# Attention on one Trainium2 core: softmax denominators by GpSimd adds and accumulating DMAs, value blocks for two steps at a time

## The chip, the cores and the metric

The kernel runs on one NeuronCore of a Trainium2 chip. The metric is the device time of one execution in microseconds (us). The kernel before has three timed runs: 3693.86, 3694.41 and 3703.93 us, median 3694.41.

## What is computed

The whole kernel is a graph attention layer followed by a transformer block on x of shape (2, 2048, 512), float32. The change touches the transformer's attention alone: 2 batches, 16 heads of 32 columns, sequences of 2048, softmax over all 2048 keys.

```python
def attention(h, Wqkv, bqkv, Wproj, bproj):
    qkv = (h @ Wqkv + bqkv).reshape(B, L, 3, H, HD)
    q, k, v = jnp.moveaxis(qkv, 2, 0)
    attn = jax.nn.softmax(jnp.einsum('blhd,bmhd->bhlm', q, k) * HD ** (-0.5), axis=-1)
    return jnp.einsum('bhlm,bmhd->blhd', attn, v).reshape(B, L, D) @ Wproj + bproj
```

## The kernel before

The program runs in phases with barriers between them: setup, graph layer, query/key/value projection, attention (`attention_phase`, line 926), output projection, MLP. Queries and keys arrive in DRAM as a high and a low float32r part (`qk_d`), so that one matmul over 3 x 32 rows gives a product of full precision.

**Groups, halves, steps.** The attention goes over 16 groups of two heads of one batch. A group has two halves of 1024 queries; a half has 16 steps of 128 keys, so a group has 32 steps (`ST`). A step computes four score tiles of 128 keys x 512 queries (two heads, two columns of queries; line 1261) into three PSUM banks `pS` used in turn. ScalarE takes the exponential of each into `prob` (line 1104), four buffers of 128x4x512 (`PR`). TensorE multiplies the values with the four tiles into one PSUM bank `pO`, four column groups of 32 (line 1228, `values`). This is a float32 product, which the trace records as eight matmuls for a block of four.

**Maxima.** The exponential needs the maximum of each query's row. So all scores are also computed the other way around, queries on the partitions, 128 tiles a group (line 1213, `maxima`), into three PSUM banks `pM`; VectorE reduces each (line 1147). These tiles belong to the next group and run 6 steps ahead of it (`LEAD`): each score matmul is followed by one maxima matmul. At step 26 VectorE takes the top of each row (line 1151), TensorE turns it (line 1219), VectorE splits it (lines 1158 and 1160), and SP sends it into two rows of `qs` (`rows`, line 1038), where it is part of the next group's contraction. TensorE begins a group only when these rows have landed (line 1267). The last group has no maxima beside it after its first steps.

**Denominators.** Of the 16 steps of a half, 11 (`ADDED`, line 944) are added up by GpSimd into `acc`: ten additions of 128x2048 (line 1083). The other five (`SUMMED`) go through TensorE, which multiplies them with a matrix of ones into the PSUM bank `pZ` right behind their values (line 1234, called from `behind`, line 1280). At step 2 of the next half (`FINISH`) the accumulator goes the same way (`finish`, line 1238). ScalarE copies the bank to `rec` (line 1133), VectorE inverts it in four pieces of 128 columns (line 1169, steps 4 to 7) and multiplies it with the copy `oc` of the values' bank (lines 1119 and 1177). ScalarE's queue stores the product with four DMAs (line 1126).

**Order and queues.** Each engine works its instructions in the order written. On TensorE a step is three scores with maxima, then the values of the step before (`behind`), then the fourth score. ScalarE may reuse a `prob` buffer once its values and its addition are done (`free`, line 1088). SP issues the loads of a group's queries and keys into one of four buffers (`U`, lines 1025 and 1028) when the group before has ended, the values' load (line 1032), and the rows. The 16 groups are written as four groups, a loop of two turns of four, and four groups (`groups`, line 1005).

Of the kernel before, what the change touches and what calls it, by code (L numbers as in the profile page):

```python
# [5 lines left out]
F32 = mybir.dt.float32  # L6
# [6 lines left out]
P = 128  # L13
B = 2
# [911 lines left out]
def attention_phase(nc, io, keep):  # L926

    with ExitStack() as ctx:
# [6 lines left out]
        MS = NM // ST  # L938
        LEAD = 6
        EARLY = MS  # L940
        U = 4
        PR = 4

        ADDED = [0, 1, 2, 4, 5, 6, 8, 9, 11, 12, 13]
        NA = len(ADDED) - 1
        FINISH = 2
        INVERT = 4
        STORE = 10
        SUMMED = [t for t in range(MT) if t not in ADDED]
# [14 lines left out]
        zero = m.sb("zero", [P, 1])  # L964
# [6 lines left out]
        top_ready, nm_hi, step_done, added, o_done, o_copied = [  # L971
            m.sem(x) for x in ("top_ready", "nm_hi", "step_done", "added", "o_done", "o_copied")]
        z_done, z_read, inverted, o_ready = [m.sem(x) for x in ("z_done", "z_read", "inverted", "o_ready")]
        top_rows = m.sems("top_rows", U)
        block = m.block()
# [6 lines left out]
        def m_unit(g, step, c):  # L982


            ahead = 1 if step < ST - LEAD else 2
            return (g + ahead, (step + LEAD) % ST * MS + c) if before(g, NG - ahead) else None

        def turn(g):


            return g * (NM + 1) + NM + (EARLY if before(g, NG - 1) else 0)

        def tile(g, n):

            return g * (NM + 1) + n - (1 if n < EARLY and at_least(g, 1) else 0)

        def bank(g, n):
            return pM[(n - (1 if n < EARLY and at_least(g, 1) else 0)) % 3]

        def turned(g):  # L1000

            return pM[(NM + (EARLY if before(g, NG - 1) else 0)) % 3]
        assert (NM + 1) % 3 == 0

        def groups(eng, body):


            for g in range(U):
                body(g, g, lambda j: (g + j) // 2)
            with eng.Fori(1, NG // U - 1) as i:  # L1010
                for k in range(U):
                    body(i * U + k, k, lambda j: i * (U // 2) + (k + j) // 2)
# [758 lines left out]
```

## Time and profile before

| | |
|---|---|
| median of three runs | 3694.41 us |
| span of the profiled execution | 3696.8 us |
| instructions | 51173 |
| busy, whole span: TensorE, VectorE, ScalarE, GpSimd | 93%, 61%, 42%, 48% |
| attention, first exponential to last score | some 990 to 2790 us |

The profile gives the span of the profiled execution, from its first to its last instruction; a time of its own around that span is not recorded, so the span is set against the median, from which it differs by 2.4 us. PE is TensorE, DVE VectorE, ACT ScalarE, POOL GpSimd, and SP the engine that only issues DMAs; a name with q behind it (SPq) is that engine's own queue. Matmuls are pipelined: each is shown longer than the distance to the next, so the distance between starts is the price of one. "Idle before" is what the engine stood still for in front of a group, with what ended it.

### The profile page before, as it was taken

How to read it: one execution, taken by the hardware profiler on the slowest of the kernel's cores; microseconds unless marked ns; L12 is line 12 of the kernel's file. 1: busy time of each engine (PE TensorE's matmuls, PEld its weight loads, DVE VectorE, ACT ScalarE, POOL GpSimd, SP SyncE). 2: the span in 40 equal slices, each digit the busy share in tenths (PEclk: the TensorE clock that was granted, in tenths of full speed). 3: DMA queues.
4: the chain of work that ended last, by engine and by line, in shares of the span. 5: the costliest groups of instructions: out<-in, count | busy, mean ns of one | idle time of the engine just before them, and what ended most of it. 6: DMA issues, size and time to landing. Idle time of an engine off the chain costs nothing. (4 is left out here: it accounts for less than half of the span.)

```text
span 3696.8 us, 51173 instructions
## 1 busy us (share of the span) xinstructions
PE 3452.4 (93%) x17516; PEld 2197.3 (59%) x17516; DVE 2266.1 (61%) x3547; ACT 1552.4 (42%) x2751; POOL 1775.8 (48%) x527
## 2 busy tenths in 40 slices
PE   7899996997999999999999999999995779999999
PEld 6488885775544444444444444444434658888887
DVE  1378874444978788788788887887715932222222
ACT  0111114341166666666656666666662242222222
POOL 1033321001288788787887887877885500000000
PEclk9999998997699999999999999999997889999999
DMA  4122224446201222102222022200004641111100
GB/s 163 66 93 88 91 80 172 172 158 183 46 17 34 43 47 44 38 16 44 47 48 44 7 44 47 47 10 13 7 6 154 216 146 68 40 40 40 37 32 23
DMA packets 158137, 250.59 MB, mean 68 GB/s; under 512 B 46939, under 2 KB 68699, under 8 KB 151774
## 3 DMA queue, kind: packets, MB, share of 16 engines
q1 hardware_dynamic: 147166, 230.96, 21.1%
q10 hardware_dynamic: 10752, 16.79, 1.5%
q8 instruction: 128, 2.10, 0.2%
q14 instruction: 91, 0.75, 0.1%
HBM read 158.89 MB, written 88.08 MB: 67 GB/s over the span
## 5 line engine op out<-in xcount | busy, mean ns | idle before, releaser
L1147 DVE TENSOR_REDUCE att_mx<-att_pM 128x1 f32<-128x512 f32 x2048 | 1267.9, 680 | 336.2 <-PE att_pM L1213 334.0
L1104 ACT ACTIVATE att_prob<-att_pS 128x512 f32<-128x512 f32 x2048 | 1080.4, 601 | 772.8 <-PE att_pS L1261 765.2
L1083 POOL TENSOR_TENSOR att_acc<-att_acc,att_prob 128x2048 f32<-128x2048 f32 x288 | 1327.5, 4609 | 129.2 <-ACT att_prob L1104 104.1
L1213 PE MATMUL att_pM<-att_ks,att_qs 96*128 96x512 f32 x2048 | 855.1, 432 | 54.7 <-DVE att_mx L1147 33.6
L1261 PE MATMUL att_pS<-att_qs,att_ks 98*128 98x512 f32 x2048 | 868.8, 430 | 10.2 <-ACT att_prob L1104 8.0
L1261 PEld LDWEIGHTS att_pS<-att_qs,att_ks 98*128 98x128 f32 x2048 | 386.2, 190 | 555.1 <-ACT att_prob L1104 385.7
L1228 PE MATMUL att_pO<-att_prob,att_V 128*32 128x512 f32 x4096 | 548.7, 608 | 0.7 <-ACT att_prob L1104 0.7
L1213 PEld LDWEIGHTS att_pM<-att_ks,att_qs 96*128 96x128 f32 x2048 | 405.4, 198 | 200.5 <-DVE att_mx L1147 120.3
L1627 DVE TENSOR_TENSOR mlp_us<-mlp_tu,mlp_us 128x512 fp32r<-128x512 f32 x128 | 89.7, 700 | 536.0 <-ACT mlp_us L1600 536.0
L1670 PE MATMUL mlp_pu<-mlp_hs,mlp_W 128*128 128x512 f32 x1536 | 370.7, 391 | 18.9 <-DVE mlp_W L1619 18.9
L1689 PE MATMUL mlp_pa<-mlp_W,mlp_us 128*128 128x512 f32 x1536 | 368.8, 389 | 0.0
L1670 PEld LDWEIGHTS mlp_pu<-mlp_hs,mlp_W 128*128 128x128 f32 x1536 | 289.7, 189 | 79.4 <-issue 19.2
L1612 POOL TENSOR_TENSOR mlp_hs<-mlp_hf,mlp_hs 128x512 fp32r<-128x512 f32 x32 | 41.1, 1287 | 598.6 <-ACT mlp_hs L1578 598.6
L1689 PEld LDWEIGHTS mlp_pa<-mlp_W,mlp_us 128*128 128x128 f32 x1536 | 288.5, 188 | 59.7
L1599 ACT ACTIVATE mlp_tu<-mlp_pu,keep_cols 128x512 f32<-128x512 f32 x128 | 88.2, 689 | 503.4 <-PE mlp_pu L1670 503.4
L1083 POOL TENSOR_TENSOR att_acc<-att_prob 128x2048 f32<-128x2048 f32 x32 | 146.6, 4580 | 291.5 <-ACT att_prob L1104 291.5
L921 PE MATMUL qkv_pq<-qkv_hs,qkv_W 128*128 128x512 f32 x768 | 187.3, 400 | 2.4 <-DVE qkv_hs L861 2.4
L1169 DVE RECIPROCAL att_rec<-att_rec 128x128 f32<-128x128 f32 x128 | 119.6, 940 | 105.3 <-ACT att_rec L1133 105.3
L1228 PEld LDWEIGHTS att_pO<-att_prob,att_V 128*32 128x32 f32 x4096 | 81.0, 108 | 166.6 <-issue 93.2
L1234 PE MATMUL att_pZ<-att_prob,att_ones 128*32 128x512 f32 x1280 | 166.6, 592 | 0.0
L921 PEld LDWEIGHTS qkv_pq<-qkv_hs,qkv_W 128*128 128x128 f32 x768 | 144.9, 192 | 32.4 <-issue 2.8
L1062 POOL MEMSET att_ones<- 128x32 f32 x1 | 0.1, 124 | 304.8 <-POOLq L107 304.8
(181 smaller groups left out, 2984.7 us busy)
## 6 DMA issues: line engine op xcount, KB each, us to landing
qk_d<-qkv_qs SPq DMA_DIRECT2D x64, 512.0 KB, 2.7
att_qs<-qk_d SPq DMA_DIRECT2D x48, 512.0 KB, 7.4
att_ks<-qk_d SPq DMA_DIRECT2D x48, 512.0 KB, 13.8
gat_xT<-in_xT SPq DMA_DIRECT2D x32, 256.0 KB, 3.1
gat_xrow<-in_x SPq DMA_DIRECT2D x32, 256.0 KB, 2.8
x_d<-gat_x SPq DMA_DIRECT2D x32, 256.0 KB, 2.1
qkv_xr<-x_d SPq DMA_DIRECT2D x8, 1024.0 KB, 5.8
v_d<-qkv_vs SPq DMA_DIRECT2D x32, 256.0 KB, 2.0
```

The source lines that it names most:

```text
L921: last = nc.tensor.matmul(out[:], a, r, start=n + c == 0, stop=n == 2 and c == DC - 1)
L1083: nc.gpsimd.tensor_tensor(acc[half][:], old[:], new[:], ALU.add).then_inc(added, 1)
L1104: nc.scalar.activation(prob[step % PR][:, c, :], pS[n % 3][:], ACT.Exp, scale=SCALE).then_inc(exp_done, 1)
L1147: nc.vector.tensor_reduce(mx[:, n // 4, n % 4:n % 4 + 1], bank(g, n)[:], AX.X, ALU.max).then_inc(m_read, 1)
L1169: nc.vector.reciprocal(rec[:, at], rec[:, at]).then_inc(inverted, 1)
L1213: nc.tensor.matmul(bank(g, n)[:], qs[k][0:KD, h, t * P:(t + 1) * P], ks[k][0:KD, h, mc * 512:(mc + 1) * 512], start=True, stop=True).then_ ...
L1228: last = nc.tensor.matmul(pO[c * HD:(c + 1) * HD, :], V[k % 2][:, mt, (c // 2) * HD:(c // 2 + 1) * HD], prob[step % PR][:, c, :], start=mt ...
L1234: last = nc.tensor.matmul(pZ[c * HD:(c + 1) * HD, :], ones[:], src[:, c, :], start=first, stop=last_one, skip_group_check=True)
L1261: nc.tensor.matmul(pS[n % 3][:], ks[k][:, h, mt * P:(mt + 1) * P], qs[k][:, h, lc * 512:(lc + 1) * 512], start=True, stop=True).then_inc(s ...
L1627: nc.vector.tensor_tensor(us[j % 2][:, 1, :], tu[j % 2][:], us[j % 2][:, 0, :], ALU.subtract).then_inc(u_lo, 1)
L1670: last = nc.tensor.matmul(pu[j % 4][:], W1[:, k, c, j * P:(j + 1) * P], hs[s][:, w, c, :], start=q + c == 0, stop=q == 2 and c == DC - 1)
L1689: last = nc.tensor.matmul(pa[nt][:], us[j % 2][:, k, nt * P:(nt + 1) * P], W2[:, w, j, :], start=j + q == 0, stop=j == MC - 1 and q == 2)
```

## The change

It does this, all in `attention_phase`:

- The steps of a half that TensorE summed are gone. Six steps of 16 (`SENT`: 2, 4, 6, 8, 10, 12) are summed by DMAs into a new tile `gathered`: the first by a plain copy on SP's queue (`send_first`), the other five by accumulating DMAs that GpSimd issues (`send`), each waiting for the one before. GpSimd adds the other ten steps (nine additions of 128x2048). `finish` moves from step 2 to step 4 of the next half and puts both `gathered` and `acc` through the ones, into a bank of the scores' turn; `pZ` goes.
- The reciprocal is packed: after ScalarE's copy SP moves one row for each of four column groups into `packed` (128x16), VectorE inverts this (step 6), SP writes it to a small DRAM tensor `z_d` and reads it back spread over 32 partitions each (`reciprocals`).
- The product with the values moves from VectorE to GpSimd (`scale`, after its fifth addition), the stores from ScalarE's queue to SP's.
- TensorE does the values of two steps together, every second step, behind the third score.
- The maxima have four PSUM banks instead of three. `prob` has eight buffers instead of four, `qs` and `ks` three each instead of four.
- The groups are written out without a loop, with constants for every wait.

```diff
+        U = 3
+        PR = 8
+        SENT = [2, 4, 6, 8, 10, 12]
+        ADDED = [t for t in range(MT) if t not in SENT]
+        FINISH = 4
+        INVERT = 6
+        SCALED = 5
...
+        gathered = m.sb("gathered", [P, 4, 512])
+        packed = m.sb("packed", [P, 16])
-        pM = [m.ps(f"pM{i}") for i in range(3)]
-        pO, pZ = m.ps("pO"), m.ps("pZ")
+        pM = [m.ps(f"pM{i}") for i in range(4)]
+        pO = m.ps("pO")
...
+            def send_first(n):
+                step = n % 2 * MT + SENT[0]
+                sp.wait_ge(exp_done, exps(n // 2, step))
+                if n >= 1:
+                    sp.wait_ge(exp_done, turns_of[n - 1] + 1)
+                sp.dma_start(gathered[:], prob[step % PR][:]).then_inc(first_sent, 16)
+            def reciprocals(n):
+                sp.wait_ge(exp_done, turns_of[n] + 1)
+                for c in range(4):
+                    row = rec[c * HD:c * HD + 1, :].rearrange("a (i x) -> a i x", x=16)
+                    sp.dma_start(packed[c * HD:(c + 1) * HD, :], row).then_inc(z_packed, 16)
+                sp.wait_ge(inverted, n + 1)
+                sp.dma_start(io["z_d"][n % 2].rearrange("c (i x) -> (c i) x", x=16), packed[:]).then_inc(z_kept, 16)
+                sp.wait_ge(z_kept, 16 * (n + 1))
+                for c in range(4):
+                    sp.dma_start(rec[c * HD:(c + 1) * HD, :], io["z_d"][n % 2, c:c + 1, :].to_broadcast([HD, 512])).then_inc(z_spread, 16)
...
+            for g in range(NG):
+                if g >= 1:
+                    sp.wait_ge(step_done, g * ST)
+                    if g + 2 < NG:
+                        load(g + 2)
+                    if g + 1 < NG:
+                        load_v(g + 1)
+                    send_first(2 * g)
+                    reciprocals(2 * g - 1)
+                    store(2 * g - 1)
+                else:
+                    send_first(0)
+                send_first(2 * g + 1)
+                reciprocals(2 * g)
+                store(2 * g)
+                if g + 1 < NG:
+                    rows(g + 1)
...
+            def send(n, j):
+                step = n % 2 * MT + SENT[j]
+                pool.wait_ge(exp_done, exps(n // 2, step))
+                if j == 1:
+                    pool.wait_ge(first_sent, (n + 1) * 16)
+                else:
+                    pool.wait_ge(sent, (n * (len(SENT) - 1) + j - 1) * 16)
+                nc.gpsimd.dma_start(gathered[:], prob[step % PR][:], accum_op=ALU.add).then_inc(sent, 16)
...
+                        nc.gpsimd.tensor_tensor(acc[half][:], old[:], new[:], ALU.add).then_inc(added, 1)
+                        if ADDED[i] - 1 in SENT[1:]:
+                            send(n, SENT.index(ADDED[i] - 1))
+                        if i == SCALED and n >= 1:
+                            pool.wait_ge(added, n * NA + i)
+                            scale(n - 1)
...
+            def finish(n):
+                at = turns_of[n]
+                pe.wait_ge(exp_done, at - 2)
+                pe.wait_ge(sent, (n + 1) * (len(SENT) - 1) * 16)
+                sums(pS[at % 3], gathered, True, False)
                 pe.wait_ge(added, (n + 1) * NA)
-                sums(acc[(step // MT - 1) % 2], False, True).then_inc(z_done, 1)
+                sums(pS[at % 3], acc[n % 2], False, True).then_inc(s_done, 1)
...
+                    for c in range(4):
+                        scores(g, step, c)
+                        if c == 2 and step % 2 == 0 and (g or step):
+                            behind(*divmod(g * ST + step - 2, ST))
+                            behind(*divmod(g * ST + step - 1, ST))
+                            if step % MT == FINISH and (g or step >= MT):
+                                finish(2 * g + step // MT - 1)
```

## Rows read from the trace of the kernel before

**Rows 1.** The page's part 1: busy time, share of the span, instructions.

```profile
PE 3452.4 (93%) x17516; PEld 2197.3 (59%) x17516; DVE 2266.1 (61%) x3547; ACT 1552.4 (42%) x2751; POOL 1775.8 (48%) x527
```

**Rows 2.** Windows, 1278 to 1390 us: busy by engine, clock, DMA share.

```profile
1278.00:1390.00 112.00, 109.66 (x605) 53.55 (x601) 91.20 (x141) 69.67 (x131) 91.08 (x21) 1.00 0.18 39
```

**Rows 3.** Timeline of ACT: copies of the values' bank, start and duration.

```profile
1101.85 0.60 ACT L1119 ACTIVATE att_oc<-att_pO 128x512 f32<-128x512 f32 x1 [0.64 <-PE att_pO L1228]
...
1214.90 0.60 ACT L1119 ACTIVATE att_oc<-att_pO 128x512 f32<-128x512 f32 x1 [0.64 <-PE att_pO L1228]
...
1838.03 0.60 ACT L1119 ACTIVATE att_oc<-att_pO 128x512 f32<-128x512 f32 x1 [0.59 <-PE att_pO L1228]
...
1898.32 0.60 ACT L1119 ACTIVATE att_oc<-att_pO 128x512 f32<-128x512 f32 x1 [1.49 <-PE att_pO L1228]
...
2634.16 0.60 ACT L1119 ACTIVATE att_oc<-att_pO 128x512 f32<-128x512 f32 x1 [0.53 <-PE att_pO L1228]
...
2785.24 0.60 ACT L1119 ACTIVATE att_oc<-att_pO 128x512 f32<-128x512 f32 x1 [1.19 <-PE att_pO L1228]
```

**Rows 4.** Timeline of PE, 1829.90 to 1834.84 us, maxima left out.

```profile
1829.90 1.06 PE L1228 MATMUL att_pO<-att_prob,att_V 128*32 128x512 f32 x8
1830.90 0.50 PE L1261 MATMUL att_pS<-att_qs,att_ks 98*128 98x512 f32 x1
...
1831.47 0.39 PE L1261 MATMUL att_pS<-att_qs,att_ks 98*128 98x512 f32 x1
...
1831.94 0.40 PE L1261 MATMUL att_pS<-att_qs,att_ks 98*128 98x512 f32 x1
...
1832.41 0.41 PE L1261 MATMUL att_pS<-att_qs,att_ks 98*128 98x512 f32 x1
...
1832.98 1.06 PE L1228 MATMUL att_pO<-att_prob,att_V 128*32 128x512 f32 x8
1833.86 1.04 PE L1234 MATMUL att_pZ<-att_prob,att_ones 128*32 128x512 f32 x8
1834.84 0.50 PE L1261 MATMUL att_pS<-att_qs,att_ks 98*128 98x512 f32 x1
```

**Rows 5.** Groups by line (busy, mean ns), and tile att_o (ns min/median/max).

```profile
L1169 DVE RECIPROCAL att_rec<-att_rec 128x128 f32<-128x128 f32 x128 | 119.6, 940 | 105.3 <-ACT att_rec L1133 105.3
...
L1612 POOL TENSOR_TENSOR mlp_hs<-mlp_hf,mlp_hs 128x512 fp32r<-128x512 f32 x32 | 41.1, 1287 | 598.6 <-ACT mlp_hs L1578 598.6
...
L1177 DVE TENSOR_TENSOR att_o<-att_oc,att_rec x32: 692/3036/4677, 1072.8 to 2796.1; 128x512 f32<-128x512 f32 x32
```

**Rows 6.** Timeline: runs on ACT, DVE and POOL, start and duration.

```profile
1803.56 2.06 ACT L1104 ACTIVATE att_prob<-att_pS 128x512 f32<-128x512 f32 x4 [1.01 <-PE att_pS L1261]
...
1804.11 2.42 DVE L1147 TENSOR_REDUCE att_mx<-att_pM 128x1 f32<-128x512 f32 x4
...
1854.36 23.51 POOL L1083 TENSOR_TENSOR att_acc<-att_acc,att_prob 128x2048 f32<-128x2048 f32 x5 [2.09 <-ACT att_prob L1104]
```

**Rows 7.** DMA issues (KB, us to landing), and GB/s in 2800 to 2830.

```profile
att_ks<-qk_d SPq DMA_DIRECT2D x48, 512.0 KB, 13.8
...
o_d<-att_o ACTq DMA_DIRECT2D x128, 64.0 KB, 1.7
...
prj_xr<-x_d SPq DMA_DIRECT2D x8, 1024.0 KB, 10.4
x_d<-prj_x SPq DMA_DIRECT2D x8, 1024.0 KB, 5.3
...
att_qs<-att_nm SPq DMA_DIRECT2D x32, 16.0 KB, 2.1
...
GB/s 0 0 66 243 298 415 306 404 410 412 352 363 382 415 402 374 309 407 366 344 380 380 412 393 186 33 0 0 0 0 0 0 0 22 0 0 0 0 0 0
```

**Rows 8.** Timeline, 2791 to 2801 us: the attention phase's end.

```profile
2791.92 0.60 ACT L1133 ACTIVATE att_rec<-att_pZ 128x512 f32<-128x512 f32 x1 [6.09 <-PE att_pZ L1234]
...
2800.90 0.37 SPq L1335 DMA_DIRECT2D prj_stage<-in_Wproj  x1
```

More of the change, by code:

```diff
@@ L980, in attention_phase, with m_tile @@
         o_v = io["o_d"].rearrange("(g h p) (b n) -> g h p b n", h=2, p=HD, b=B)
-        def m_unit(g, step, c):
+        def m_tile(g, step, c):
             ahead = 1 if step < ST - LEAD else 2
-            return (g + ahead, (step + LEAD) % ST * MS + c) if before(g, NG - ahead) else None
-        def turn(g):
[L991 to L1012, printed above, removed]
-            for g in range(NG - U, NG):
-                body(g, g % U, lambda j: (g + j) // 2)
@@ L1016, in half_before, with fill @@
-        def half_before(g, step):
-            return 2 * g + step // MT - 1
+            return (g + ahead, (step + LEAD) % ST * 4 + c) if g + ahead < NG else None
+        place = {}
+        def fill(what):
+            place[what] = len(place)
+        for q in range(NM):
+            fill((0, q))
+        for q in range(EARLY):
+            fill((1, q))
+        fill("turned 0")
+        for q in range(EARLY, LEAD * 4):
+            fill((1, q))
+        for g in range(NG):
+            for step in range(ST):
+                if step == ST - LEAD + 1 and g + 1 < NG:
+                    fill(f"turned {g + 1}")
+                for c in range(4):
+                    if m_tile(g, step, c):
+                        fill(m_tile(g, step, c))
@@ new lines, in attention_phase, with score_turn, exps @@
+        turns_of = {}
+        def score_turn(what):
+            turns_of[what] = len(turns_of)
+        for g in range(NG):
+            for step in range(ST):
+                for c in range(4):
+                    score_turn((g, step, c))
+                    if c == 2 and step % MT == FINISH and (g or step >= MT):
+                        score_turn(2 * g + step // MT - 1)
+        score_turn(2 * NG - 1)
+        def exps(g, step):
+            return turns_of[g, step, 3] + 1
+        def turn(g):
+            return place[f"turned {g}"]
@@ new lines, in _ @@
+            load(0)
+            load(1)
+            load_v(0)
+            load_v(1)
+            load(2)
+            rows(0)
+            for g in range(NG):
+                if g >= 1:
+                    sp.wait_ge(step_done, g * ST)
+                    if g + 2 < NG:
[12 more added lines that the diff above has]
+                    rows(g + 1)
@@ L1060, in _ @@
+            reciprocals(2 * NG - 1)
+            store(2 * NG - 1)
+            for x in o_stored:
+                sp.wait_ge(x, 16 * 4 * NG)
         @block.gpsimd
@@ L1269, in body @@
+            for q in range(NM):
+                maxima(0, q)
+            for q in range(EARLY):
+                maxima(1, q)
+            top_of(0)
+            for q in range(EARLY, LEAD * 4):
+                maxima(1, q)
+            pe.wait_ge(cleared, 1 + U)
+            for g in range(NG):
+                pe.wait_ge(top_rows[g % U], (g // U + 1) * 32)
+                pe.wait_ge(v_loaded[g % 2], (g // 2 + 1) * 16)
                 for step in range(ST):
-                    if step == ST - LEAD + 1 and before(g, NG - 1):
+                    if step == ST - LEAD + 1 and g + 1 < NG:
```

331 lines of the change are left out of this document (144 added, 187 removed).

## The prediction

> **What bounds the kernel now.** I read the busy times of the page first: TensorE has work in 93% of the span [rows 1]. Busy is not yet bound, so next came the windows. In a 112 us stretch of the attention loop TensorE is busy 109.7 us, VectorE 91.2, GpSimd 91.1 and ScalarE 69.7, at full clock [rows 2]. TensorE is first there and two others are close enough to take over.
>
> The copies of the values' bank (one for each half group, 32 in all) give the rhythm: 1214.90 - 1101.85 = 113.05 us for a group, **56.5 us for a half** of 16 steps. One half, around 1898, took 60.3 us; the last three together took 151.1 us, without maxima for most of them [rows 3]. From 1101.85 to 2634.16 lie 27 halves, 1532.3 us, which is 27 x 56.5 and some 6 to 7 more; with the half before 1101.85 I count 28 of full rhythm.
>
> The timeline of TensorE shows what a half is made of [rows 4]. A plain step is 1832.98 - 1829.90 = 3.08 us: values to first score 1.00, first to second score 0.57, two more at 0.47 (each with a maxima matmul between), last score to values 0.57. So in a run a score with its maxima costs 0.47, and a change of kind adds 0.10 behind the first score and 0.10 ahead of the values. Values followed by ones matmuls take 0.88 instead of 1.00, the ones 0.98. A half is then 16 x 3.08 = 49.3, plus five ones blocks of 0.86 (4.3), plus one closing block of some 1.1: 54.7. The other 1.8 us are VectorE's: a reciprocal of 0.94 us [rows 5] on top of four maxima (2.42 us, 0.605 each [rows 6]) makes 3.36 us, over the 3.08 of a step, four times (1.1 us); and the product that ends the half takes 3.04 us in the median where it can take 0.69 [rows 5].
>
> GpSimd adds at 23.51 / 5 = 4.70 us and still waits for ScalarE before its runs [rows 6], so it does not bind now.
>
> **The change, part by part.**
>
> *TensorE.* Values now come for two steps at a time: eight scores with maxima, then two value blocks. Gap by gap: 0.57 + 6 x 0.47 + 0.57 + 0.88 + 1.00 = 5.84 us for two steps, 46.7 for a half. The five ones blocks go; the closing one becomes two (accumulator and gathered block): 2 x 0.98, less 0.12 because the values before them are followed by their own kind. **TensorE's path: 48.6 us** [rows 4]. Two conditions: eight maxima at 0.605 are 4.84 us and eight exponentials at 2.06 / 4 = 0.515 are 4.12 [rows 6], both inside 5.84. Within the run, maxima leave TensorE every 0.47 and VectorE takes 0.605: the eighth tile asks for its bank at 7 x 0.47 = 3.3 us, and the fourth of four banks is read at some 0.4 + 4 x 0.605 = 2.8, so four banks cover it; with three it would be the fifth tile's read, 3.4, a small stall. That is what the freed bank is worth, some 0.1 us a run, and the sum has no such stall.
>
> *VectorE.* Four reciprocals of 0.94 us become one of 128x16, and the product leaves: 3.8 + 3.0 us a half off an engine that then holds 64 x 0.605 = 38.7. It is out of the race.
>
> *GpSimd.* Ten adds become nine: 9 x 4.70 = 42.3. It takes the product: the nearest row is a 128x512 operation of two inputs on this engine, 1.29 us [rows 5]. It issues five accumulating DMAs. No row has an issue on this engine. From below 0.37 us, an issue on SP's queue [rows 8]; from above the 1.29 of the small product, since this engine would write the transfer's list as it works through a tile. I take 1.0, nearer to the row of the same engine: 5.0. **GpSimd's own work: 48.6 us**, as much as TensorE's.
>
> *The chain of accumulating DMAs.* This decides. Each of the five waits for the landing of the one before, and the wait stands in GpSimd's own order, so it holds back the adds behind it. The order is add 1, 3, 5, send, add 7, send, add 9, send, product, add 11, send, add 13, send, add 14, 15. Between first and last send are four intervals, each as long as the larger of the landing L and about 5.7 (add plus issue; 7.0 once, with the product). Outside are five adds, 23.5, and one issue, 1.0. So **a half is at least 24.5 + 4 L**. It equals TensorE's 48.6 at L = 6.0, and today's 56.5 at L = 8.0. No row has a DMA from SBUF to SBUF, nor one that adds. Bounds: 1024 KB plain, one way, lands in 5.3 us (store in the projection); in a crowd, 10.4 [rows 7]. A value from rows: an addition must read both operands, 2.1 MB; the best slices of the projection's start move 412 to 415 GB/s [rows 7], which makes 5.1 us, and the 64 KB store's 1.7 us less its own 0.2 is the fixed part: L = 6.6. I take that, since it is nearer to the 5.3 of the same size on an empty queue than to the crowded 10.4. Then a half is 24.5 + 26.4 = **50.9 us**, 5.6 less than now.
>
> *SP's queue.* It gets the first plain copy of a half (1 MB, landing 5.3), four packing DMAs, one to DRAM, four back, the stores, and, behind those, the top rows of the next group. A small DMA lands in 2.1 us [rows 7]. The first copy goes at step 4 behind the closing sums, lands two steps later and is asked for after add 5, 14.1 us behind them: hidden. The three hops of the denominators (some 9 us with issues) end before the product, which waits for the third send: hidden. The top rows come last: product done 14.1 + 2 x 6.6 + 2 x 1.0 + 1.3 = 30.6 us behind the closing sums, four stores and two row DMAs issued at 0.37 each, landing 2.1: 34.9; TensorE comes to the next group after 11.3 steps x 2.92 = 33.0 us. It would wait 1.9 us a group. That costs nothing while GpSimd is last, as TensorE has 2.3 us to spare each half; with that cover gone it is 15 x 1.9 = 28 us. The same holds for the key and query loads, which crowd the queues for the first five steps of a group and may lengthen the last send.
>
> *Three buffers for keys instead of four, eight for probabilities instead of four.* The load for group g+2 starts at the start of g and is asked for 26 steps (some 75 us) later; its pieces of 512 KB land in 13.8 us in the median [rows 7]. Nothing. Eight blocks let GpSimd be late by up to four steps more, which it needs.
>
> *Loops written out.* The long half of 60.3 is where the loop turns, 3.8 us over the rhythm; with its entry and exit it is the 7 us over 27 x 56.5 [rows 3]. They go.
>
> **Sum, against the span of 3696.8**, which is 2.4 us over the median of 3694.4: 28 halves x 5.6 = -157; loop edges -7; first half, where GpSimd is not yet late, -8; last three halves 3 x 50.9 = 152.7 against 151.1, +2; the end: sums to the next phase's first load takes 2800.90 - 2791.92 = 9.0 us now [rows 8], and the reciprocals' 3.5 are replaced by three hops with issues (about 9) and a slower product, +7. Together -163: 3534 against the span, **3531** against the median.
>
> **The rivals.**
> 1. *The DMAs are quick and nothing of the chain shows (L up to 6).* TensorE and GpSimd tie at 48.6: 28 x 7.9 = -221, -7, -8, last three 145.8 against 151.1 -5, end +7: -234, so 3460. For it: no DRAM at either end, so L may lie at the 5.3 of the plain store. Against: two operands to read. The Trainium skill ("DMA: Bandwidth & Descriptors", Anatomy of one DMA) gives 2.0 us plus the bytes at 436 GB/s for a DMA of this queue, 4.4 us for 1 MB, which would put the kernel into this case; this trace's plain megabyte took 5.3, and no run so far has an accumulating one.
> 2. *Slower: the chain outgrows the half.* Place: GpSimd's wait ahead of each send. If the two operands are read one behind the other at the pace of one plain megabyte, L = 1.7 + 2 x (5.3 - 1.7) = 8.9 and the half is 60.1: 28 x 3.6 = +101, last three 180.3 against 151.1 +29, loop edges -7, end +7: 3824. It decides from L = 8.0 up. For it: each landing comes with an issue by GpSimd of unknown price, and loads share the engines once a group. Against: TensorE saves nothing that this takes until L passes 8.
> 3. *The work moved off TensorE was hidden anyway.* Then the time would stay. Against: TensorE's idle in a steady half is 2% [rows 2], so its 5 blocks are on the path. Only a mix near L = 8 gives no change.
>
> **Chances.** Forecast (chain binds, L 6.0 to 7.8, time 3470 to 3670): 0.40. Rival 1: 0.31. Rival 2: 0.25. No change: 0.04. A difference under about 0.3% (11 us) can't be told from none here. Faster 0.71, same 0.04, slower 0.25. The range goes from 3450 (rival 1, with the loop edges and a little more) to 3770 (a half of 58.5, L = 8.5), which leaves out the worst of rival 2, some 0.15.
>
> **What would show it.** Copies of the values' bank 51 us apart instead of 56.5. On TensorE pairs of value blocks, 5.84 us from pair to pair where nothing waits, and no ones matmuls on probabilities. On GpSimd: sends 6.6 us apart, its idle time ahead of the adds put down to a DMA; TensorE waiting at the closing sums of each half for GpSimd. VectorE under 40 us busy a half. If sends stand under 6 us apart and TensorE never waits, rival 1 holds; over 8, rival 2. The forecast would be wrong at its root if TensorE's pairs took over 6.1 us, or if GpSimd's adds slowed beside the DMAs from 4.70.

## The result, and the profile after

The changed kernel takes 3750.6 us in the median of four runs (3742.9 to 3758.5), the kernel before 3699.2 in the runs beside it: ratio 1.0135, 95% interval 1.0113 to 1.0157. It is slower by 1.4%, where 3531 and a gain were forecast. The time lies inside the stated range (3450 to 3770), near its upper end, but on the other side of the kernel before: the forecast gain did not come. The one that comes near is rival 2.

The page's first part, and the line of its second part that shows the granted clock of TensorE in tenths, to be read against [rows 1]:

```profile
PE 3334.6 (89%) x16492; PEld 2225.5 (59%) x16492; DVE 2056.1 (55%) x3419; ACT 1527.7 (41%) x2751; POOL 1800.3 (48%) x685
...
PEclk8999998997699999999899999999987889999999
```

TensorE's share falls from 93% to 89% while the span grows: it waits. The window of one group in the middle of the attention (columns as in [rows 2]) says the same; the DMA engines' share goes from 0.18 to 0.68.

```profile
1795.10:1911.30 116.20, 104.32 (x546) 55.80 (x546) 79.74 (x133) 68.42 (x133) 93.72 (x31) 0.94 0.68 150
```

The copies of the values' bank, as in [rows 3]:

```profile
1795.06 0.60 ACT L1186 ACTIVATE att_oc<-att_pO 128x512 f32<-128x512 f32 x1 [2.94 <-PE att_pO L1286]
...
1850.52 0.60 ACT L1186 ACTIVATE att_oc<-att_pO 128x512 f32<-128x512 f32 x1 [1.31 <-PE att_pO L1286]
...
1911.27 0.60 ACT L1186 ACTIVATE att_oc<-att_pO 128x512 f32<-128x512 f32 x1 [2.78 <-PE att_pO L1286]
```

The two halves take 55.5 and 60.8 us. Over 26 halves, from the copy at 1102.60 to the one at 2611.24, a half takes **58.0 us** in the mean, against 56.8 for the same 26 before. The difference of the two spans can be added up from this. By its second copy the attention is 0.8 us later, 26 x 1.25 = 32.5 us come in these halves, 2.9 in the last four, and the stretch from the last copy to the next phase's first load grows from 15.7 to 36.2 us, by 20.5. The phases behind give back 2.7. The sum is 54.0, as 3750.8 - 3696.8.

TensorE's timeline, maxima left out as in [rows 4]:

```profile
1887.67 0.50 PE L1316 MATMUL att_pS<-att_qs,att_ks 98*128 98x512 f32 x1
...
1891.89 1.92 PE L1286 MATMUL att_pO<-att_prob,att_V 128*32 128x512 f32 x16
1893.75 0.50 PE L1316 MATMUL att_pS<-att_qs,att_ks 98*128 98x512 f32 x1
...
1897.69 1.92 PE L1286 MATMUL att_pO<-att_prob,att_V 128*32 128x512 f32 x16
1899.54 0.50 PE L1316 MATMUL att_pS<-att_qs,att_ks 98*128 98x512 f32 x1
...
1906.08 0.50 PE L1316 MATMUL att_pS<-att_qs,att_ks 98*128 98x512 f32 x1 [3.93 <-DMA att_qs<-att_nm]
...
1928.35 1.94 PE L1292 MATMUL att_pS<-att_gathered,att_ones 128*32 128x512 f32 x8 [5.55 <-ACT att_prob L1203]
```

The new order runs as worked out: 3.94 us from the first score of a run to the values (3.96), 1.85 for two value blocks (1.88), 5.79 from pair to pair (5.84). But at 1906.08 TensorE has stood 3.93 us for the top rows, and at 1928.35 another 5.55 ahead of the closing sums, behind ScalarE. Its own work is short enough; something else sets the half.

Behind such a wait TensorE also runs slower for a while. Two stretches of 4 us, at and behind an earlier wait of the changed kernel (TensorE busy, granted clock, DMA share, GB/s):

```profile
1807.00:1811.00 4.00, 0.00 (x0) 1.00 1.06 221
1811.00:1815.00 4.00, 3.80 (x17) 0.57 0.97 205
```

The clock falls from the upper of its two levels (2.4 GHz, shown as 1.00) towards the lower (1.2 GHz, 0.50) behind 4 us without a matmul. Over 1102 to 2550 us its mean is 1.00 before and 0.94 now. The next timeline shows why this does not set the half either. It is GpSimd's:

```profile
1880.34 0.86 POOL L1134 DMA_DIRECT2D att_gathered<-att_prob  x1
1880.95 4.89 POOL L1154 TENSOR_TENSOR att_acc<-att_acc,att_prob 128x2048 f32<-128x2048 f32 x1
1888.51 0.89 POOL L1134 DMA_DIRECT2D att_gathered<-att_prob  x1 [2.67 <-DMA att_gathered<-att_prob]
...
1896.02 0.88 POOL L1134 DMA_DIRECT2D att_gathered<-att_prob  x1 [2.02 <-ACT att_prob L1203]
1896.63 1.59 POOL L1124 TENSOR_TENSOR att_o<-att_oc,att_rec 128x512 f32<-128x512 f32 x1
...
1903.79 0.88 POOL L1134 DMA_DIRECT2D att_gathered<-att_prob  x1 [0.87 <-DMA att_gathered<-att_prob]
...
1911.28 0.87 POOL L1134 DMA_DIRECT2D att_gathered<-att_prob  x1 [2.05 <-DMA att_gathered<-att_prob]
1911.89 9.64 POOL L1154 TENSOR_TENSOR att_acc<-att_acc,att_prob 128x2048 f32<-128x2048 f32 x2
...
1936.11 4.58 POOL L1154 TENSOR_TENSOR att_acc<-att_acc,att_prob 128x2048 f32<-128x2048 f32 x1 [5.28 <-ACT att_prob L1203]
1940.64 0.87 POOL L1134 DMA_DIRECT2D att_gathered<-att_prob  x1
```

Sends start at 1880.34, 1888.51, 1896.02, 1903.79 and 1911.28, some 7.5 to 8.2 us apart. An issue followed by an add is over in 5.5 (1880.34 to 1880.95 to 1885.8), and then GpSimd stands. The profile puts one of these waits down to the landing of the send before (2.67), another to ScalarE (2.02). The landing times show that it is the landing each time: in 126 of the 128 intervals of the trace the next send starts 0.53 to 0.56 us behind the landing of the one before, whichever the profile names. A later TensorE or ScalarE therefore does not lengthen these intervals. Over the 26 halves counted above, the four intervals of a half have means of 8.2, 8.0, 8.0 and 7.7 us. From the last send of a half to the first of the next pass 24.3 us inside a group and 27.9 across a group's start. Together that is the half of 58.0. The last halves, with no key or query load beside them, come nearest to a floor: 7.5, 7.5, 7.8, 7.5 and 24.2, **54.5 us**.

The DMAs of the changed kernel (KB, median us from issue to landing, over the kernel), and two of its waits (us in total, times, longest):

```profile
att_gathered<-att_prob POOLq DMA_DIRECT2D x160, 1024.0 KB, 7.2
...
att_gathered<-att_prob SPq DMA_DIRECT2D x32, 1024.0 KB, 4.7
...
o_d<-att_o SPq DMA_DIRECT2D x128, 64.0 KB, 4.7
...
ACT att_prob L1203 <- DMA att_gathered<-att_prob: 172.7, 53, 9.4
POOL att_gathered L1134 <- DMA att_gathered<-att_prob: 161.5, 79, 4.5
```

The 64 KB stores, 1.7 us on ScalarE's queue before [rows 7], take 4.7 on SP's. What the DMA engines carry beside a send shows in its landing. Of the 104 sends inside these 26 halves that another send follows, 43 had under 100 KB of SP's transfers beside them and landed in 7.0 us in the mean, and 30 with more of these landed in 7.5. With a packet of the queue that the profile calls q8 instruction beside them, 18 took 7.8, and 13 that met both took 8.2. This is a sorting of one trace, not a test.

The half that crosses into a new group is different. Here are SP's queue, ScalarE, and the landing of the last send of that half (columns of the three: start, duration, or KB and us to landing):

```profile
1898.25 4.18 SPq L1059 DMA_DIRECT2D o_d<-att_o  x4
1902.48 1.19 SPq L1050 DMA_DIRECT2D att_qs<-att_nm  x2
1911.26 1.28 SPq L1038 DMA_DIRECT2D att_qs<-qk_d  x3
1912.59 1.84 SPq L1040 DMA_DIRECT2D att_ks<-qk_d  x3
```

```profile
1927.70 1.57 ACT L1203 ACTIVATE att_prob<-att_pS 128x512 f32<-128x512 f32 x3 [7.62 <-DMA att_gathered<-att_prob]
```

```profile
att_gathered<-att_prob POOLq DMA_DIRECT2D x1, 1024.0 KB, 16.3
```

The top rows go out at 1902.48, behind the stores, and TensorE waits for them. It comes to the new group at 1906; with that the loads of keys and queries start, at 1911.26, in the same moment as the last send at 1911.28. That send takes 16.3 us instead of 7.2. ScalarE may not overwrite its block before, stands 7.62 us, and GpSimd's third add of the next half begins 5.28 late. In the 13 crossings that have such loads this send lands in 12 to 17 us, 15.0 in the mean.

The end of the phase:

```profile
2821.39 0.60 ACT L1186 ACTIVATE att_oc<-att_pO 128x512 f32<-128x512 f32 x1 [1.19 <-PE att_pO L1286]
...
2843.00 2.41 SPq L1074 DMA_DIRECT2D att_packed<-att_rec  x4
...
2857.60 0.41 SPq L1387 DMA_DIRECT2D prj_stage<-in_Wproj  x1
```

From the copy of the values' bank to the copy of the sums (2842.38) pass 21.0 us, where it was 6.7 before: GpSimd has two sends and three additions left when TensorE has finished the values, and nothing covers them here.

### The profile page after: what moved, and what is told of

It reads as the page before. It is cut to its first block and busy times, and to the rows that moved or that the text cites. A ratio compares the mean times of both kernels' runs of the same rounds, so it can differ in the third digit from the quotient of the medians.

```text
span 3750.8 us, 44693 instructions
## 1 busy us (share of the span) xinstructions
PE 3334.6 (89%) x16492; PEld 2225.5 (59%) x16492; DVE 2056.1 (55%) x3419; ACT 1527.7 (41%) x2751; POOL 1800.3 (48%) x685
## 3 DMA queue, kind: packets, MB, share of 16 engines
q1 hardware_dynamic: 174814, 281.84, 24.5%
## 5 line engine op out<-in xcount | busy, mean ns | idle before, releaser
L1218 DVE TENSOR_REDUCE att_mx<-att_pM 128x1 f32<-128x512 f32 x2048 | 1254.7, 681 | 517.9 <-PE att_pM L1271 517.4
L1203 ACT ACTIVATE att_prob<-att_pS 128x512 f32<-128x512 f32 x2048 | 1054.1, 615 | 718.6 <-PE att_pS L1316 542.3
L1154 POOL TENSOR_TENSOR att_acc<-att_acc,att_prob 128x2048 f32<-128x2048 f32 x256 | 1204.8, 4706 | 56.0 <-ACT att_prob L1203 39.7
L1316 PEld LDWEIGHTS att_pS<-att_qs,att_ks 98*128 98x128 f32 x2048 | 394.3, 193 | 472.1 <-issue 203.1
L1286 PE MATMUL att_pO<-att_prob,att_V 128*32 128x512 f32 x4096 | 524.8, 632 | 0.0
L1271 PEld LDWEIGHTS att_pM<-att_ks,att_qs 96*128 96x128 f32 x2048 | 414.7, 203 | 154.9 <-DVE att_mx L1218 78.1
L1134 POOL DMA_DIRECT2D att_gathered<-att_prob x160 | 139.9, 875 | 282.2 <-DMA att_gathered<-att_prob 161.5
L1286 PEld LDWEIGHTS att_pO<-att_prob,att_V 128*32 128x32 f32 x4096 | 110.7, 113 | 266.3 <-ACT att_prob L1203 136.8
L1513 PE MATMUL prj_pp<-prj_W,prj_os 128*128 128x512 f32 x384 | 99.1, 422 | 49.0 <-POOL prj_os L1462 49.0
```

Source lines behind the costliest of these rows:

```text
L1134: nc.gpsimd.dma_start(gathered[:], prob[step % PR][:], accum_op=ALU.add).then_inc(sent, 16)
L1154: nc.gpsimd.tensor_tensor(acc[half][:], old[:], new[:], ALU.add).then_inc(added, 1)
L1203: nc.scalar.activation(prob[step % PR][:, c, :], pS[at % 3][:], ACT.Exp, scale=SCALE).then_inc(exp_done, 1)
L1218: nc.vector.tensor_reduce(mx[:, q // 4, q % 4:q % 4 + 1], bank(at)[:], AX.X, ALU.max).then_inc(m_read, 1)
L1271: nc.tensor.matmul(bank(at)[:], qs[k][0:KD, h, t * P:(t + 1) * P], ks[k][0:KD, h, mc * 512:(mc + 1) * 512], start=True, stop=True).then_in ...
L1286: last = nc.tensor.matmul(pO[c * HD:(c + 1) * HD, :], V[g % 2][:, mt, (c // 2) * HD:(c // 2 + 1) * HD], prob[step % PR][:, c, :], start=mt ...
```

## The experiments

Each one is an edit of the changed kernel; the diffs show their main lines. There are two theories. **C**: the chain of accumulating DMAs sets the half, and the loads lengthen its last link. **R**: the rows' place on SP's queue is what costs. Ratios are to the kernel before, run beside.

**e1: rows ahead of the stores.**

```diff
                 reciprocals(2 * g)
-                store(2 * g)
                 if g + 1 < NG:
                     rows(g + 1)
+                store(2 * g)
```

> The changed kernel with one thing moved on SP's queue: the top rows of the next group go out ahead of the stores. In the changed kernel's trace TensorE stands 83.8 us in all for these rows at the 15 group starts. Theory R (the rows' place on the queue is the loss, what turns a half of 56.6 into one of 58): those waits go and the kernel takes about 3700 us. Theory C (the half is set by GpSimd's chain of sends, the loads at a group's start lengthening the last one): the waits for the rows go, but TensorE waits as long at the closing sums instead, and the time stays within 15 us of 3750.

Measured: 3818.3 us, ratio 1.0323 (1.0300 to 1.0347). Slower by 68 us than with the rows late, which neither theory had. TensorE's waits for the rows are gone, and the halves alternate between 55.2 and 65.4 us, where the changed kernel's do between 56.7 and 59.3. SP's queue and GpSimd's fourth and fifth send of one crossing show why:

```profile
1817.36 1.43 SPq L1038 DMA_DIRECT2D att_qs<-qk_d  x3
1818.83 1.67 SPq L1040 DMA_DIRECT2D att_ks<-qk_d  x3
...
1818.72 0.87 POOL L1134 DMA_DIRECT2D att_gathered<-att_prob  x1 [0.92 <-DMA att_gathered<-att_prob]
1819.33 4.88 POOL L1154 TENSOR_TENSOR att_acc<-att_acc,att_prob 128x2048 f32<-128x2048 f32 x1
1836.48 0.88 POOL L1134 DMA_DIRECT2D att_gathered<-att_prob  x1 [12.27 <-DMA att_gathered<-att_prob]
```

TensorE now starts the group earlier and brings the loads along: they go out at 1817.4 to 1820.5, around the fourth send at 1818.72, and not at the fifth. GpSimd waits 12.27 us for its landing, and the fifth follows after 17.8 us instead of 7.5 (10.7 to 18.1 in the 13 groups with loads). The fifth itself, which the loads hit in the changed kernel, has adds behind it before the next send is due. On this reading the late rows had been shielding the chain in the changed kernel. R falls. C had forecast a time within 15 us of 3750 and missed it too; that the rows act as a switch for when the loads come is an explanation made after the run, and e5 tests it.

**e2: loads apart from the chain.** The queries' and the keys' loads now wait for different sends; `load` issues either.

```diff
                     sp.wait_ge(step_done, g * ST)
+                    sp.wait_ge(sent, 2 * g * (len(SENT) - 1) * 16)
                     if g + 2 < NG:
-                        load(g + 2)
+                        load(g + 2, (0,))
...
+                sp.wait_ge(sent, (2 * g + 1) * (len(SENT) - 1) * 16)
+                if g >= 1 and g + 2 < NG:
+                    load(g + 2, (1,))
                 send_first(2 * g + 1)
```

> The changed kernel with the key and query loads moved: the queries and values of a group wait on SP for the last send of the half before, the keys for the last send of the next half, so that no load shares the DMA engines with that send. Theory C: the last send of every second half lands in 7 to 8 us instead of 16, ScalarE no longer waits some 7 us a group for its buffer, a group crossing costs 24.3 us from last to first send instead of 27.7: 15 x 3.4 = 50 us less, 3700. Against it: the first copy of a half then queues behind the loads and the first send comes later, which gives the gain back (3750 or more). Theory R: no gain, since the rows are as late as before.

Measured: 3702.0 us, ratio 1.0004 (0.9990 to 1.0017); 49 us less than the changed kernel, as expected. The gap from last to first send is 24.3 us in every half now; the mean half is 55.9 instead of 58.0. So the loads' meeting with the last send is worth 49 us, nearly the whole loss against before (51).

**e3: sends as plain copies.** The kernel leaves out the five additions inside the DMAs of a half, so each send overwrites `gathered` and five of the six sent steps are missing from the denominators (the expectation says four).

```diff
-                nc.gpsimd.dma_start(gathered[:], prob[step % PR][:], accum_op=ALU.add).then_inc(sent, 16)
+                nc.gpsimd.dma_start(gathered[:], prob[step % PR][:]).then_inc(sent, 16)
```

> The changed kernel with the five sends of a half as plain copies: the addition inside the DMA is left out (so the denominators lack four steps of a half), number, size, issuing engine and waits stay. Theory C: a plain megabyte lands in 4.7 to 5.3 us, under the 5.6 of an add and an issue, so the chain drops out; sends stand 5.7 us apart (7.5 once, with the product), a half falls from 58 to 49 or 51 and the time to 3480 to 3540. If what holds the half is not the length of the chain but the number of DMAs or GpSimd's work, the time falls by less than 60 us.

Measured: 3506.6 us, ratio 0.9481 (0.9458 to 0.9503). The landing of the sends, and the windows of a half inside a group and one across:

```profile
att_gathered<-att_prob POOLq DMA_DIRECT2D x160, 1024.0 KB, 4.7
...
1847.90:1896.20 48.30, 48.30 (x274) 27.07 (x275) 39.95 (x68) 33.59 (x66) 46.82 (x16) 1.00 0.42 154
1896.20:1948.10 51.90, 49.95 (x273) 27.63 (x274) 39.20 (x65) 33.82 (x67) 45.22 (x16) 0.97 0.69 203
```

A megabyte lands in 4.7 us without the addition and in 7.2 with it, on the same engines and from the same issuer. With 4.7 TensorE is busy all of the 48.3 us of an undisturbed half, and 48.6 had been its sum. 244 us hang on 2.5 us of landing in each send: the chain is the bound, as C says. That it is the waiting, and not the DMAs' traffic, is left to the runs with two chains (e6, e9), whose sends land no faster.

**e4: no sends, the six steps through TensorE.**

```diff
-        pM = [m.ps(f"pM{i}") for i in range(4)]
-        pO = m.ps("pO")
+        pM = [m.ps(f"pM{i}") for i in range(3)]
+        pO, pZ = m.ps("pO"), m.ps("pZ")
...
-                values(g, step).then_inc(step_done, 1)
+                last, t = values(g, step), step % MT
+                if t in SENT:
...
+                    last = sums(pZ, prob[step % PR], t == SENT[0], False)
+                last.then_inc(step_done, 1)
```

Not shown: `finish` is back at step 2 and adds into `pZ`, and the first copies and ScalarE's waits for the sends are gone.

> The changed kernel without sends: the six steps of a half that the DMAs added go through TensorE with the ones matrix, into a bank of their own, which leaves three banks for the maxima; value blocks for two steps, packed reciprocal, product on GpSimd and written-out groups stay. TensorE's sum: 8 x 5.84 + 6 x 0.98 + 0.98 = 53.6 us a half; GpSimd has 9 x 4.7 + 1.6 = 44. So a half of 53.6 to 54.5, 28 x 2 to 2.9 less than before and the loop edges: 3600 to 3650, faster than both kernels. If the pairs of value blocks or the packed reciprocal cost what the chain seems to cost, it stays at 3700 or more.

Measured: 3698.8 us, ratio 0.9996 (0.9983 to 1.0008), a half of 55.9. It misses the upper end of the expected by 49 us. TensorE's timeline and its waits for the maxima's banks (us in total, times, longest):

```profile
1901.71 0.50 PE L1307 MATMUL att_pS<-att_qs,att_ks 98*128 98x512 f32 x1
...
1906.05 1.06 PE L1274 MATMUL att_pO<-att_prob,att_V 128*32 128x512 f32 x8
1906.94 1.04 PE L1280 MATMUL att_pZ<-att_prob,att_ones 128*32 128x512 f32 x8
1907.80 1.04 PE L1274 MATMUL att_pO<-att_prob,att_V 128*32 128x512 f32 x8
1908.77 0.50 PE L1307 MATMUL att_pS<-att_qs,att_ks 98*128 98x512 f32 x1
```

```profile
PEld att_pM L1259 <- DVE att_mx L1206: 254.8, 941, 0.4
```

Nothing of the chain is left, and the ones cost 0.86 a block as in [rows 4]. But the run of eight scores takes 4.34 us instead of 3.94. The reading is that on three banks the last tiles go at VectorE's pace of 0.61. That is 8 x 0.4 = 3.2 us a half, and it takes back what the pairs of value blocks give.

**e8: e3 with three banks** tests that reading where nothing else differs from e3.

```diff
-        pM = [m.ps(f"pM{i}") for i in range(4)]
+        pM = [m.ps(f"pM{i}") for i in range(3)]
```

> e3 (the addition inside the DMA left out, 3507 us) with three PSUM banks for the maxima instead of four. In e4 a run of eight scores took 4.34 us on three banks, against 3.96 in the changed kernel on four. If this is the banks' price, a half of e3 (48.3 between group crossings) becomes 48.3 + 8 x 0.38 = 51.3 and the time 3507 + 30 x 2.5 to 3.0 = 3580 to 3600. If it belonged to e4's ones blocks, the time stays within 15 us of 3507.

Measured: 3583.4 us, ratio 0.9696 (0.9672 to 0.9720), 77 us over e3, as expected.

```profile
PEld att_pM L1271 <- DVE att_mx L1218: 273.5, 953, 1.9
```

The fourth bank is worth 77 us once value blocks come in pairs, and it is there because the sums no longer hold a bank of their own.

**e5: e1 and e2 together.**

```diff
+                    sp.wait_ge(sent, 2 * g * (len(SENT) - 1) * 16)
...
-                store(2 * g)
                 if g + 1 < NG:
                     rows(g + 1)
+                store(2 * g)
```

> Both edits of e1 and e2 together: rows ahead of the stores, and the loads bound to the last send of a half. e1 alone was 3818, e2 alone 3702, the changed kernel 3751. Theory C says that e1 was slower because an earlier group start brought the loads forward, onto the fourth send of a half, which has no adds behind it to hide in; with the loads bound to the last send that can't happen, so the rows' edit costs nothing here and may give back part of TensorE's 49 us of waits: 3670 to 3705. If sending the rows early is bad in itself (its stores come later, or TensorE runs ahead into full buffers), it costs again some 68 us: 3770.

Measured: 3698.1 us, ratio 0.9999 (0.9986 to 1.0012), equal to e2 and as expected. With the loads tied down, rows early or late make no difference, where without that e1 had cost 68 us: the 49 us that TensorE waits for the rows in e2 were covered.

**e6: two chains** (e1's edit too).

```diff
-        gathered = m.sb("gathered", [P, 4, 512])
+        gathered = [m.sb(f"gathered{i}", [P, 4, 512]) for i in range(2)]
-        o = [m.sb(f"o{i}", [P, 512]) for i in range(2)]
+        o = [rec, rec]
...
-                if j == 1:
-                    pool.wait_ge(first_sent, (n + 1) * 16)
+                if j <= 3:
+                    pool.wait_ge(first_sent[j % 2], (n + 1) * 16)
                 else:
-                    pool.wait_ge(sent, (n * (len(SENT) - 1) + j - 1) * 16)
+                    pool.wait_ge(sent[j % 2], (n * 2 + 1) * 16)
```

> The changed kernel with two gathered tiles: the blocks of steps 2, 6, 10 and 4, 8, 12 are summed apart, the first of each by a plain copy on SP's queue, so a send waits for the one before the last and four sends are left; the closing sums get one block more (0.97 us); rows ahead of the stores; to make room the product is written in place of the reciprocals. Theory C: no send waits any more, TensorE with 48.3 + 1.0 = 49.3 us or GpSimd with 9 x 4.7 + 1.6 + 4 x 0.6 = 46.3 sets the half, with some 2 us at group crossings for the loads: a half of 50 to 51.5, 3500 to 3560, faster than both kernels. If accumulating DMAs are limited by their bytes over the 16 engines and not by each one's landing, two at a time land in twice the time and it stays above 3650.

Measured: 3634.6 us, ratio 0.9840 (0.9812 to 0.9868). Faster than both kernels, yet 75 us short of the expected. The halves alternate between 51.6 and 57.6 us. VectorE's timeline in one of the long ones:

```profile
1880.21 0.69 DVE L1218 TENSOR_REDUCE att_mx<-att_pM 128x1 f32<-128x512 f32 x1 [0.92 <-PE att_pM L1271]
1887.15 0.25 DVE L1237 RECIPROCAL att_packed<-att_packed 128x16 f32<-128x16 f32 x1 [6.25 <-DMA att_packed<-att_rec]
```

The reciprocal at step 6 waits for the packed sums, whose DMAs queue on SP behind two first copies and the loads. The maxima stand behind it, and TensorE behind them (5.72 us here). The sends themselves wait no more for each other: of GpSimd's 161.5 us of waiting for landings none is left at the sends.

**e7: two chains, rows behind the stores**, which is e6 with e1's edit taken back.

```diff
-                if g + 1 < NG:
-                    rows(g + 1)
                 store(2 * g)
+                if g + 1 < NG:
+                    rows(g + 1)
```

> e6 with the rows behind the stores, as in the changed kernel. With the half set by TensorE its waits for the rows are no longer covered: I worked out 1.9 us a group before the run of the changed kernel, its trace showed 5.6. Theory C: e7 is slower than e6 by 15 x 2 to 6 us, 30 to 85 us. If the rows' place costs only through the loads that follow it, e7 equals e6 or is faster.

Measured: 3640.4 us, ratio 0.9837 (0.9804 to 0.9869), the same as e6, so the 30 to 85 us that theory C gave did not come. Here too something else held the crossing half, VectorE's wait (57.6 us in e6 and e7 alike). TensorE, held by it, comes so late that it waits under 1 us in all for the rows, so this run does not price them.

**e9: e6 with the reciprocal at step 9.**

```diff
-        INVERT = 6
-        SCALED = 5
+        INVERT = 9
+        SCALED = 6
```

> e6 with VectorE's reciprocal at step 9 instead of 6 and GpSimd's product one addition later. In e6's trace a half inside a group takes 50.6 us, but the one that crosses a group 57.8: behind the loads on SP's queue the packed sums come late, VectorE stands 6.2 us in front of the reciprocal with the maxima behind it, and TensorE waits for its banks (97 us in all). Theory C with this wait as the rest: the crossing half falls to 51 to 53, 14 x 5 to 6.5 = 70 to 90 us less: 3545 to 3565. If the crossing is long because the loads slow the sends, the reciprocal's step changes less than 15 us.

Measured: **3515.3 us, ratio 0.9502** (0.9474 to 0.9530), 5.0% faster than the kernel before. The gain over e6 is 119 us, more than the 70 to 90 expected; a crossing half falls from 57.6 to 49.7. Behind e6's waits TensorE also ran at the lower clock (0.50 in 1888 to 1892, after 5.72 us of standing), and its mean clock over 1102 to 2550 us rises from 0.96 to 0.99, which the expectation had not counted; how much of the rest it explains is not measured. Window of a whole group, the sends' landing, and ScalarE's wait for them:

```profile
1746.20:1845.90 99.70, 98.52 (x562) 55.02 (x563) 79.09 (x133) 67.27 (x133) 91.78 (x30) 1.00 0.76 175
...
att_gathered<-att_prob POOLq DMA_DIRECT2D x128, 1024.0 KB, 7.9
...
ACT att_prob L1203 <- DMA att_gathered<-att_prob: 12.0, 3, 7.7
```

TensorE is busy 98.5 of 99.7 us at full clock. A send takes 7.9 us in the median, longer than before, but GpSimd never waits for one, ScalarE 12.0 us in all instead of 172.7, and TensorE 5.5.

**e10 and e11: the late reciprocal on one chain**, alone and with e2's edit.

```diff
-        INVERT = 6
-        SCALED = 5
+        INVERT = 9
+        SCALED = 6
```

> The changed kernel with the late reciprocal alone, one chain. Its trace shows VectorE's wait for the packed sums in 10 of 32 halves only, and TensorE ahead of GpSimd all the time, so theory C says the wait is covered: 3735 to 3755. If VectorE's wait was part of what made the changed kernel slower, the time falls by 30 us or more.

> e2 (loads bound to the last send, 3702) with the late reciprocal. In e2 VectorE waited for the packed sums in 27 halves, 207 us in all, 53 of them ahead of the first one and at the end. If that is what keeps e2 over the floor of one chain (54.5 us a half, the last undisturbed halves of the changed kernel), the mean half falls from 56.1 to about 54.7: 3655 to 3670. If e2's rest is the first copy behind the loads (7.6 us to landing instead of 4.7), nothing changes: 3690 to 3705.

Measured: 3796.0 us, ratio 1.0254 (1.0236 to 1.0272), and 3768.3 us, ratio 1.0182 (1.0163 to 1.0200). Both were to be equal or faster, and both are slower, by 45 and 66 us. TensorE's wait for the rows in e11 (us in total, times, longest):

```profile
PE att_pS L1320 <- DMA att_qs<-att_nm: 201.8, 15, 14.4
```

The later product moves the stores, and with them the rows: 13.5 us a group where the changed kernel had 5.6. That is no longer covered, and behind each of these waits the clock is low: in 1924 to 1928 it is 0.50, and the 16 matmuls of a pair of value blocks at 1926.31 take 3.62 us instead of 1.92. Moving the rows ahead gives back 40 of the 66 us (e12 below), so the rows are harmless only up to some point between 5.6 and 13.5 us.

**e12: one chain with all three moves**: e1's and e2's diffs and the late reciprocal.

```diff
-        INVERT = 6
-        SCALED = 5
+        INVERT = 9
+        SCALED = 6
...
+                    sp.wait_ge(sent, 2 * g * (len(SENT) - 1) * 16)
...
-                store(2 * g)
                 if g + 1 < NG:
                     rows(g + 1)
+                store(2 * g)
```

> The changed kernel with all three moves (rows ahead of the stores, loads bound to the last send, late reciprocal) and still one chain of five sends: everything on the queues is out of its way, so what is left is the chain alone. Theory C: four intervals of 7.5 and 24.3 us around them, 54.3 to 54.8 us a half, in every half: about 40 us under e5's 3698, 3650 to 3670, and 140 above e9, whose only difference in kind is the second chain. If the queues still hold it, it stays at 3690 or more; if it comes near e9's 3515, the chain was never the floor.

Measured: 3727.9 us, ratio 1.0068 (1.0046 to 1.0089). The rows' waits are gone, and with them 40 us of e11. Against e5, which lacks the late reciprocal alone, it is 30 us slower. But it misses the expected 3650 to 3670: a half is no 54.5 but 56.8. Over the same 26 halves the send intervals have means of 7.9, 8.8, 7.9 and 7.9, with 24.3 between halves. The second interval has grown, and it is there that the reciprocals' way back from DRAM now lies. The interval is 9.1 us in the 15 halves in which the rows go out then too and 8.3 in the others, against 7.8 in e2. That these small transfers lengthen it is argued from their place, not tested. What is shown: none of the seven kernels with one adding chain came below 3698; with two chains and the late reciprocal it was 3515. e9 and e12 stand some 210 us apart, with the same late reciprocal and early rows. They differ in the second chain, in one send less by GpSimd, and in the loads, which e9 does not even tie down.

## Why the prediction was wrong

The direction was wrong, though the mechanism, the chain of sends, was the right one.

- **TensorE's path** (48.6 us a half): right. 48.3 in e3 where nothing waits, 5.79 a pair.
- **GpSimd's own work** (48.6): near. Adds 4.7 as taken, the product 1.6 for 1.29; an issue holds the engine for 0.6 us (1880.34 to 1880.95), not 1.0. Some 47.
- **The chain: the step that failed.** The form (24.5 + 4 L) was right, the term L was mis-sized. L was put at 6.6 us. A send lands in 7.2 us in the median and in 6.9 at the least, and the 0.5 us from a landing to the next send had been put at nothing: 7.5 from send to send where nothing disturbs it. That alone lifts the half from 50.9 to 54.5. I had read a peak of 412 GB/s off other transfers [rows 7] and let both operands flow at it. By the prediction's own sum 54.5 still gives some 3643 us, a gain; its condition for the forecast (L from 6.0 to 7.8) was met, its time was not.
- **"The same holds for the key and query loads", priced at nothing.** This is the second failure, and the one that turns the gain into a loss. A chain without slack takes every delay of every link. The four intervals are 31.9 us instead of 30.3, since landings get longer beside other DMAs (the sorting above), and the loads at the last send add 3.6 us at each group's start, 1.8 a half (e2: 49 us). 54.5 + 1.6 + 1.8 = 57.9, against 58.0 measured. In the prediction's sum these 3.4 us in 28 halves turn 3643 into 3738; the 14 us left out at the end (below) make it 3752. That this meets 3750.6 so closely is luck, since the -8 us of the first half did not come. I had named the 10.4 us of a crowded megabyte as a bound and then used the one of an idle queue, for a kernel whose DMA engines turned out 68% busy.
- **Rival 2** had the right mechanism and place. It was to decide from L = 8.0 up, and no undisturbed landing is that long (7.2 in the median); but the mean interval, with the 0.5 us and the crowd in it, is 8.0, by its own formula 24.5 + 4 x 8.0 = 56.5, and the crossing does the rest. Its price of 3824 was too high.
- **Rival 1** is what e3 shows: 3507, for the 3460 worked out.
- **The end** (+7 us): right for what it counted, 9.0 us from the copy of the sums to the next load before [rows 8] and 15.2 now. Left out was GpSimd's lag behind TensorE, from the values' copy to the sums' copy 21.0 us instead of 6.7: 20.5 us in all. That eight buffers let this lag grow was not tested.
- **The first half** (-8 us): it did not come. The first copy of the values' bank is 3.3 us earlier than before, the second already 0.8 later.
- **The rows** (1.9 us a group, covered): 5.6 in the trace, and covered (e5 against e2). That their lateness also held the loads back from the chain I had not seen.
- **The fourth bank** ("some 0.1 us a run"): 0.4 us a run, 77 us in all (e8).

Two rules of the Trainium skill stand beside this. "DMA: Bandwidth & Descriptors" (Anatomy of one DMA) gives 2.0 us plus the bytes at 436 GB/s, 4.4 us for a megabyte; e3's plain copies took 4.7, near it. The Trainium skill's "Collectives: The Full Stack" (The bandwidth ceiling) says of the ReduceScatter among several cores, not of a DMA inside one, that its add is slow because it reads two sources through one ring, and not because adding takes time. Carried over to these sends it would double the moving part, an estimate of 6.8 us by both pages; the trace has 7.2. The packets agree with the doubling: one of 8 KB takes 0.64 us in the median with the addition and 0.33 in e3's plain copies. Which part of that is the second read no run separates.

## What to carry to other kernels

A series of DMAs that each wait for the one before is a path of its own: put it beside the engines' sums with the landing time of that very kind of transfer, and of a busy queue, before trusting that it hides. Cut in two (e9), the chain was no longer waited for, though its transfers landed no faster. And when a wait disappears, ask what starts earlier: here the rows' wait was covered, and taking it away sent the group's loads into a link that had no slack. A wait that nothing covers costs TensorE twice, once for standing and once for the lower clock behind it (e11).

## What the runs showed of the hardware

- From SBUF to SBUF, 1 MB of 8 KB rows lands in 4.7 us as a copy, from either queue, and in 7.2 us as a float32 addition; beside 3.5 MB of loads in 12 to 17. The next transfer that waits for it is issued 0.5 us behind the landing.
- GpSimd is held 0.6 us by the issue of an accumulating DMA of 128 rows, though the trace shows the instruction as 0.88.
- A 128x512 product on VectorE with both operands in SBUF took 3.04 us in the median beside GpSimd's adds and 0.69 at best [rows 5]; on GpSimd it takes 1.3 to 1.6.
- 128x16 reciprocals take 0.24 us against 0.94 for 128x128. They save VectorE 3.5 us a half, but placed where VectorE had to wait for them they cost 119 us (e6 to e9, which also moves GpSimd's product by one addition).
- TensorE ran no matmul in 1807 to 1811 us of the changed kernel, and its granted clock was 0.57 in the 4 us behind. At 0.50 (1.2 GHz) 16 value matmuls took 3.62 us (e11), at 1.00 (2.4 GHz) 1.92.
